# Local attention: the inverse roots on ScalarE and GpSimd without powers, and half of the probabilities' division on GpSimd

## What is computed

```
qkv = shift_token(x) @ wqkv
q, k, v = split(qkv, 3)                      # 8 heads of 64
q = q / clip(norm(q), 1e-12) * q_scale
k = k / clip(norm(k), 1e-12) * k_scale
q, k = rotary_xpos(q, k)                     # q * cos * s + rotate_half(q) * sin * s, k with 1 / s
sim = (q * 8) @ k.T  for windows of 64 queries, 128 keys (the window and the one before)
attn = softmax(where(mask, -max, sim))
x = x + (attn @ v) @ wo
```

## Time and profile before

| | us |
|---|---|
| median of 3 runs (790.19 to 793.98) | 792.9 |
| the profiled execution | 794.17 |
| its span, first to last instruction | 792.4 |
| mean granted TensorE clock, share of full speed | 0.938 |

### The profile page before, as it was taken

One profiled execution on the slowest core, in us unless ns is written; L12 is line 12 of the kernel. 1 busy time (PEld: TensorE's weight loads), 2 busy tenths in 40 slices (PEclk: granted clock), 3 DMA queues, 4 the chain that ended last, 5 costly groups with the idle time before them and its releaser, 6 DMA issues. The chain is left out here.

```text
span 792.4 us, 15860 instructions
## 1 busy us (share of the span) xinstructions
PE 630.7 (80%) x5506; PEld 438.3 (55%) x5539; DVE 569.8 (72%) x1440; ACT 489.6 (62%) x1423; POOL 391.0 (49%) x436
## 2 busy tenths in 40 slices
PE   1747778778999986986899998699699999997242
PEld 0425555345666664553567666555477777776112
DVE  2454666878999974645999998555577777777396
ACT  1524666576889973324989998432577777774243
POOL 6626665798999941109999997010101111111202
PEclk9887999999999999998999999999999999998665
DMA  6700000001001001011001101000000000000001
GB/s 201 163 1 1 1 1 1 8 21 22 22 22 34 22 22 58 1 27 24 22 21 28 23 22 25 11 1 1 1 1 2 1 1 3 1 2 1 1 0 53
DMA packets 20218, 17.26 MB, mean 22 GB/s; under 512 B 7234, under 2 KB 15884, under 8 KB 20044
## 3 DMA queue, kind: packets, MB, share of 16 engines
q1 hardware_dynamic: 20140, 16.26, 8.3%
HBM read 8.91 MB, written 1.05 MB: 13 GB/s over the span
## 5 line engine op out<-in xcount | busy, mean ns | idle before, releaser
L1131 ACT ACTIVATE pc<-PS,nb,rsq 128x128 f32<-128x128 f32 x256 | 114.1, 464 | 2.7 <-DVE nb L1469 2.1
L761 PE MATMUL PS<-wqkv,hB 128*128 128x512 f32 x192 | 104.9, 631 | 8.0 <-DVE rsin L1455 4.8
L1189 ACT ACTIVATE pc<-PS,nb 128x256 f32<-128x256 f32 x128 | 59.0, 473 | 45.0 <-DVE nb L1619 45.0
L450 POOL TENSOR_TENSOR rsk<-btmp,neghalf 128x8 f32<-128x8 f32 x32 | 60.5, 1890 | 5.9 <-POOL btmp L445 5.9
L769 PEld LDWEIGHTS PS<-ident,rot 128*128 128x128 f32 x256 | 31.6, 143 | 53.1 <-issue 33.7
L1619 DVE TENSOR_REDUCE nb<-PS 128x2 f32<-128x512 f32 x64 | 40.8, 680 | 25.0 <-PE PS L943 25.0
L450 POOL TENSOR_TENSOR rsq<-btmp,neghalf 128x8 f32<-128x8 f32 x32 | 53.1, 1661 | 6.2 <-POOL btmp L445 6.2
L1478 DVE TENSOR_TENSOR pc<-pc,rden 128x512 f32<-128x512 f32 x64 | 53.8, 841 | 2.2
L555 POOL TENSOR_TENSOR rot<-rot,rsin 128x512 f32<-128x512 f32 x32 | 40.6, 1270 | 27.1 <-DVE rsin L1455 27.1
L1131 ACT ACTIVATION_READ_ACCUMULATOR pc<-PS,nb,rsq 128x1 f32 x256 | 53.8, 210 | 0.0
L769 PE MATMUL PS<-ident,rot 128*128 128x128 f32 x256 | 39.7, 279 | 16.7 <-POOL rot L561 16.2
(11 more groups left out here) (226 smaller groups left out, 1717.8 us busy)
## 6 DMA issues: line engine op xcount, KB each, us to landing
V<-V SPq DMA_DIRECT2D x48, 128.0 KB, 2.2
wqkv<-in_L_ffn_wqkv SPq DMA_DIRECT2D x2, 768.0 KB, 5.0
out<-x SPq DMA_DIRECT2D x4, 256.0 KB, 2.3
x<-in_x SPq DMA_DIRECT2D x1, 768.0 KB, 5.4
ctxT<-in_ctxT SPq DMA_DIRECT2D x1, 768.0 KB, 7.3
w<-in_L_ffn_w SPq DMA_DIRECT2D x2, 341.0 KB
ctxs<-in_ctx SPq DMA_DIRECT2D x1, 576.0 KB, 6.5
gel<-in_bands SPq DMA_DIRECT2D x1, 512.0 KB, 7.1
```

Source lines behind the costliest of these rows:

```text
L450: return tt(dst, tmp, neghalf[:, 0, 0:tmp.shape[1]], ALU.pow)
L761: i = mm(ps, hB[:, b % 2, j * P:(j + 1) * P], wqkv[:, w * INNER:(w + 1) * INNER], start=True, stop=True)
L1131: i = af(pc[:, g % 2, par, c * P:(c + 1) * P], c_bank(g, par)[:, c * P:(c + 1) * P], ACT.Exp, bias=nb[:, g % 2, at], scale=rsq[:, g % 8, 2 ...
L1189: i = af(pc[:, u % 2, par, n * S:(n + 1) * S], c_bank(u, par)[:, n * S:(n + 1) * S], ACT.Exp, bias=nb[:, u % 2, par * 2 + n:par * 2 + n + ...
```

## The change

It does five things, all in local attention. (1) The clip of the sums of squares is done for q and k at once (128x16), and ahead of both rotary sums; GpSimd waits for both sums of squares there. (2) ScalarE takes logarithm and exponential, exp(-0.5 ln s), in place of the power (`b_roots`), and GpSimd refines the result by one Newton step of four small operations, then makes the k product. (3) The division of the odd bank's probabilities moves from VectorE to GpSimd (`b_normalise`), behind `b_turned` in each step; VectorE keeps the reciprocal. (4) The order of pieces and of VectorE's and ScalarE's jobs in a step is changed: k, t, q ahead of the scores, kT, v, W, qT behind, the even bank ahead of the odd one, sums of squares ahead of the rotary products. (5) ScalarE loads one table set with logarithm and exponential at its start and at the start of layer 1.

```diff
-B_MID = ["t", "k", "kT"]
-B_END = ["v", "qT", "q", "W"]
+B_MID = ["k", "t", "q"]
+B_END = ["kT", "v", "W", "qT"]
 @@ GpSimd
             def b_turned(g):
-                _, k, turn = b_piece("k", g)
-                pool.wait_ge(bank_free[k], 2 * turn + 2)
-                r = rot[:, g % 2 * 2, :]
-                tt(r, r, rsin[:, 0, :], ALU.add).then_inc(sem("B_ksum"), 1)
                 pool.wait_ge(sem("B_kss"), g + 1)
-                rsqrt(rsk[:], ss[:, g % 2, 0, :], btmp[:, 0, :], 1e-24, ALU.max, "B_ktmp", g + 1).then_inc(sem("B_krs"), 1)
+                pool.wait_ge(sem("B_qss"), g + 1)
+                sg, r = ss[:, g % 2], rsqk[:, g % 8]
+                ts(sg, sg, 1e-24, None, ALU.max).then_inc(sem("B_clip"), 1)
+                for name in ("k", "q"):
+                    _, k, turn = b_piece(name, g)
+                    pool.wait_ge(bank_free[k], 2 * turn + 2)
+                    m = rot[:, g % 2 * 2 + int(name == "q"), :]
+                    tt(m, m, rsin[:, int(name == "q"), :], ALU.add).then_inc(sem("B_ksum" if name == "k" else "B_q"), 1)
+
+                pool.wait_ge(sem("B_root"), 2 * g + 2)
+                tt(root[:, 0], r, r, ALU.mult).then_inc(sem("B_newton"), 1)
+                pool.wait_ge(sem("B_newton"), 4 * g + 1)
+                tt(root[:, 1], root[:, 0], sg, ALU.mult).then_inc(sem("B_newton"), 1)
+                pool.wait_ge(sem("B_newton"), 4 * g + 2)
+                ts(root[:, 0], root[:, 1], -0.5, 1.5, ALU.mult, ALU.add).then_inc(sem("B_newton"), 1)
+                pool.wait_ge(sem("B_newton"), 4 * g + 3)
+                tt(r, r, root[:, 0], ALU.mult).then_inc(sem("B_newton"), 1)
+                pool.wait_ge(sem("B_newton"), 4 * g + 4)
                 pool.wait_ge(sem("B_ksum"), g + 1)
...
+                r3 = rot[:, g % 2 * 2, :].rearrange("p (h d) -> p h d", h=H)
+                tt(r3, r3, rsqk[:, g % 8, 0, :].unsqueeze(2).broadcast_to([P, H, DH]), ALU.mult).then_inc(sem("B_k"), 1)
+
+            def b_normalise(g):
+
+                pool.wait_ge(b_rden[1], g + 1)
+                e = pc[:, g % 2, 1, :].rearrange("p (n k) -> p n k", n=4)
+                tt(e, e, rden[:, g % 2, 4:8].unsqueeze(2).broadcast_to([P, 4, P]), ALU.mult).then_inc(p_full[1], 1)
+
+            def b_step(layer, step):
+
+                if 0 <= step + B_AHEAD["k"] < T:
+                    b_turned(layer * T + step + B_AHEAD["k"])
+                if 0 <= step + 1 < T:
+                    b_normalise(layer * T + step + 1)
 @@ ScalarE
+            nc.scalar.preload_act_table_set("natural_log_exp_and_others")
             act.wait_ge(sem("ld_A"), A_LOADS * 16)
...
+            def b_roots(g):
+
+                r = rsqk[:, g % 8]
+                act.wait_ge(sem("B_clip"), g + 1)
+                af(r, ss[:, g % 2], ACT.Ln).then_inc(sem("B_root"), 1)
+                act.wait_ge(sem("B_root"), 2 * g + 1)
+                af(r, r, ACT.Exp, scale=-0.5).then_inc(sem("B_root"), 1)
 @@ ScalarE, b_step
-                if ahead:
-                    b_exps(g + 1, 1)
                 if 0 <= step < T:
                     for par in range(2):
                         b_copy(g, par)
-                pieces("k", "t")
+                pieces("k")
                 if ahead:
                     b_exps(g + 1, 0)
-                pieces("kT", "v", "qT", "q")
+                pieces("q", "t")
+                if ahead:
+                    b_exps(g + 1, 1)
+                pieces("kT")
+                if 0 <= step + B_AHEAD["q"] < T:
+                    b_roots(g + B_AHEAD["q"])
+                pieces("v", "qT")
 
             for layer in range(DEPTH):
                 if layer:
+                    nc.scalar.preload_act_table_set("natural_log_exp_and_others")
 @@ VectorE: in b_turned the sum of squares (red, L1458) moves ahead of the two products
 @@ VectorE, b_scale
-                nc.vector.reciprocal(rden[:, g % 2, at], den[:, g % 2, at]).then_inc(sem("B_rden"), 1)
-                dve.wait_ge(sem("B_rden"), g * 2 + 2 - par)
+                nc.vector.reciprocal(rden[:, g % 2, at], den[:, g % 2, at]).then_inc(b_rden[par], 1)
+                if par:
+                    return
+                dve.wait_ge(b_rden[0], g + 1)
 @@ VectorE, b_step
+                if 0 <= step + B_AHEAD["k"] < T:
+                    b_turned(0, g + B_AHEAD["k"])
+                if 0 <= step + 1 < T:
+                    b_scale(g + 1, 0)
+                if 0 <= step + B_AHEAD["q"] < T:
+                    b_turned(1, g + B_AHEAD["q"])
                 if 0 <= step + 1 < T:
                     b_scale(g + 1, 1)
-                if 0 <= step + B_AHEAD["k"] < T:
-                    b_turned(0, g + B_AHEAD["k"])
                 if 0 <= step + 2 < T:
-                    b_max(g + 2, 1)
-                if 0 <= step + 1 < T:
-                    b_scale(g + 1, 0)
-                if 0 <= step + 2 < T:
-                    b_max(g + 2, 0)
+                    for par in range(2):
+                        b_max(g + 2, par)
                 if 0 <= step < T:
                     b_outputs(g)
-                if 0 <= step + B_AHEAD["q"] < T:
-                    b_turned(1, g + B_AHEAD["q"])
```

More of the change, by code:

```diff
@@ L226, in program @@
         rs = sb("rs", [P, 4])
-        rsq = sb("rsq", [P, 8, H])
-        rsk = sb("rsk", [P, H])
+        rsqk = sb("rsqk", [P, 8, 2, H])
+        root = sb("root", [P, 2, 2, H])
         av = sb("av", [P, 3, 10 * D])
@@ L294, in program @@
         bank_full, bank_free = ([sem("bank_%s%d" % (name, k)) for k in range(3)] for name in ("full", "free"))
+        b_rden = [sem("B_rden%d" % par) for par in range(2)]
         b_v2 = [sem("B_v2_%d" % k) for k in range(4)]
@@ L550, in b_turned @@
             def b_turned(g):
-                _, k, turn = b_piece("k", g)
-                pool.wait_ge(bank_free[k], 2 * turn + 2)
-                r = rot[:, g % 2 * 2, :]
-                tt(r, r, rsin[:, 0, :], ALU.add).then_inc(sem("B_ksum"), 1)
                 pool.wait_ge(sem("B_kss"), g + 1)
-                rsqrt(rsk[:], ss[:, g % 2, 0, :], btmp[:, 0, :], 1e-24, ALU.max, "B_ktmp", g + 1).then_inc(sem("B_krs"), 1)
-                pool.wait_ge(sem("B_ksum"), g + 1)
-                pool.wait_ge(sem("B_krs"), g + 1)
@@ L574, in _ @@
                         a_step(u)
-                        if 0 <= u - A_UNITS + B_AHEAD["k"] < T:
-                            b_turned(u - A_UNITS + B_AHEAD["k"])
-                else:
-                    for t in range(T):
-                        b_turned(layer * T + t)
+                        b_step(0, u - A_UNITS)
+                else:
+                    for step in B_STEPS:
+                        b_step(layer, step)
                 def f_copy(g):
@@ L1131, in b_exps @@
                     i = af(pc[:, g % 2, par, c * P:(c + 1) * P], c_bank(g, par)[:, c * P:(c + 1) * P], ACT.Exp,
-                           bias=nb[:, g % 2, at], scale=rsq[:, g % 8, 2 * c + par:2 * c + par + 1], accum_out=den[:, g % 2, at])
+                           bias=nb[:, g % 2, at], scale=rsqk[:, g % 8, 1, 2 * c + par:2 * c + par + 1], accum_out=den[:, g % 2, at])
                 i.then_inc(e_full[par], 1)
@@ L1450, in b_turned @@
                 dve.wait_ge(sem("B_%ssq" % name), g + 1)
+                red(ss[:, g % 2, which, :], sq[:, which, :].rearrange("p (h d) -> p h d", h=H), AXX, ALU.add) \
+                    .then_inc(sem("B_%sss" % name), 1)
                 tt(rot[:, g % 2 * 2 + which, :].rearrange("p (h d) -> p h d", h=H), ps.rearrange("p (h d) -> p h d", h=H),
@@ L1457, in b_turned @@
                    ALU.mult).then_inc(bank_free[k], 2)
-                red(ss[:, g % 2, which, :], sq[:, which, :].rearrange("p (h d) -> p h d", h=H), AXX, ALU.add) \
-                    .then_inc(sem("B_%sss" % name), 1)
             def b_max(g, par):
@@ L1466, in b_max @@
                     .then_inc(sem("B_mx"), 1)
-                dve.wait_ge(sem("B_mx"), g * 2 + 2 - par)
-                dve.wait_ge(sem("B_qrs"), g + 1)
-                tt(nb[:, g % 2, at], mx[:, g % 2, at], rsq[:, g % 8, par::2], ALU.mult).then_inc(nb_full[par], 1)
+                dve.wait_ge(sem("B_mx"), g * 2 + par + 1)
+                dve.wait_ge(sem("B_newton"), 4 * g + 4)
+                tt(nb[:, g % 2, at], mx[:, g % 2, at], rsqk[:, g % 8, 1, par::2], ALU.mult).then_inc(nb_full[par], 1)
             def b_scale(g, par):
```

## The result

The changed kernel takes 879.7 us (median of 4, 877.05 to 882.04) against 792.9 us before: ratio 1.107, 95% interval 1.102 to 1.111. It is slower by 87 us; the forecast was 875, inside 848 to 900. The profiled execution took 878.1 us, its span is 876.3 against 792.4.

What follows compares the result with a forecast made beforehand. GpSimd was taken to set the rate, 8.45 us a tile. With steps of 12.4 us, layer 1 +44.7, layer 0 +38.1, edges +1.2 and table -1.3 gave +82.7 us on the 792.9 us median: 875 us, range 848 to 900.

Steps and rivals of the forecast that it cites:

- The ring: In full local-attention steps, the odd turn waits for GpSimd's division, queued behind its wait for tile g+4: 11.9 us a step.
- The clock: TensorE's idle gap in each ring step makes some matmuls run slow: +0.5 us a step, bounds 0 and 1.3.
- rival (b): TensorE's clock stays slow through all of the ring: 24x0.8 us more, 895 us; chance 0.08.
- The shared port: VectorE with two SBUF inputs and a reading GpSimd exclude each other; VectorE's products nb wait, but the sum is unchanged.
- The edges: Filling and draining of both local layers: 2x(1.1-0.5) = +1.2 us, with the early table load -1.3 us.
- draining: Last three steps of each local layer, without b_turned: 6.2 us each, 18.6 against 19.1 us, so -0.5.
- overlap of layer 0 with the first attention, 0 with +-5: Where layer 0 overlaps the first attention, steps take about 10 us either way: no change, within 5 us.
- the prediction's 10, 19 and 5 us: Upward uncertainties used for the range: Newton's operation times 10 us, the slow clock +19, layer 0's overlap +-5.
- (a): The ring without a slow clock: 24 steps of 11.9 us, 863 us; chance 0.77 together with the forecast.
- (c): Every logarithm and exponential on ScalarE loads its table: 48 us longer, 923 us; chance 0.03.
- (d): The ring has misread slack, 3.5 of 6.3 us hidden; ScalarE's 8.2 us then bounds a step: 774 us; chance 0.05.
- (e): Half of the slack in the ring is hidden: a period of 10.5 us, 830 us; chance 0.07.

## Why the prediction was right, and where it wasn't

**The ring** (its main step) was right in kind and in size. Forecast 11.9 us without the clock, measured 11.57; clip at 5.60, measured 5.63. The differences are in the Newton step, 1.19 for 1.35, since an operation takes 0.22 for 0.24 and the gap ahead of the product is 0.08 for 0.15, in the clip, 0.20 for 0.26, and in the handover from GpSimd to TensorE, 0.05 (473.51 - 472.42 - 1.04) for the 0.15 that the earlier trace rows gave. TensorE is idle for 2.8 us ahead of a turn, a little under the 3 us that the prediction named as a sign.

**The clock** was right in kind: 0.41 us a step on average for a forecast of 0.5, and the repeated transposes show that the idle gap causes it. It also settles rival (b): the clock isn't slow throughout.

**The shared port** is off the ring, as forecast. In the step shown above, VectorE's product nb that starts at 469.48, inside GpSimd's sums of 467.77 to 470.27, takes 0.81 us; the next one, outside them, takes 0.16. None of the ring's waits names it. The port comes onto the path, as far as I found, only in the run with q's sum of squares last and the division on VectorE, where that division holds up the clip.

**Sizes that were off.** With a step of 12.4 for a measured 12.0 the two layers were put 10 us too high. The edges were put 11 us too low: 5.4 in the start, 1.8 in the filling of layer 1, 3.7 in the draining. The term that failed is "overlap of layer 0 with the first attention, 0 with +-5". The trace of the changed kernel shows what it left out (timeline of all engines):

```profile
139.58 0.21 ACT L1148 ACTIVATE rsqk<-ss 128x16 f32<-128x16 f32 x1 [1.54 <-POOL ss L556]
...
142.01 1.09 PE L732 MATMUL PS<-pT,av 128*64 128x128 f32 x16 [2.71 <-ACT pT L1095]
...
147.98 1.92 PE L778 MATMUL PS<-wqkv,hB 128*128 128x512 f32 x2
```

ScalarE waits for the clip, the first attention's copies come late, TensorE idles for 2.7 us, and two of the next projections then run at the lower clock (2.07 and 1.92 us, the latter as in the earlier trace rows). The turn after comes 16.2 us later (136.79 to 152.99), 10.8 before. Every profiled kernel with the roots on ScalarE has 16 us or more there; the kernel before with the early table alone has 10.8. From the turn at 129.40 to tile 0's odd turn it is 9.8 us more than before; the start had gained 4.6 us, some by the table and the rest by a clock that fell elsewhere in this one execution. So the edges' 11 us too little and the layers' 10 us too much cancelled, and the closeness of 875 to 880 is partly luck: the ring itself accounts for 72.8 us of the 83.9. The upper end of the range isn't the sum of its parts either: 875 and the prediction's 10, 19 and 5 us make 909, not 900.

**Draining** was put at 18.6 and took 19.7 and 21.2. The last two steps are 6.3 and 6.2 us, as forecast, but the first of the three takes 7.2 and 8.7.

**The rivals.** (a) and the forecast were the case. (c), the table not kept, is ruled out: beside the start one load stands ahead of each layer or stage that changes the set, none between logarithm and exponential, which follow each other in 0.26 us. (d) and (e), slack in the ring, did not occur; but (d)'s price was too good for the kernel that it describes: once the ring is cut, the step is 8.54, not 8.2, and the best time is 787, not 774.

## What to carry to other kernels

When a job moves to another in-order engine, write down what stands ahead of it in that engine's queue, and follow each of these waits back: if one leads to the job's own consumer one step earlier, the step can't be shorter than the way round, however idle the engines are. The cure is to split the moved work so that the short thing somebody waits for goes first, and to give the buffers inside the loop a second copy: here the same instructions gave 880, 822, 810 and, with one more buffer, 787 us. And before taking work off one of several engines that are nearly full, look at what stands next to it: some 2.4 us less on GpSimd went with 0.04 us less in a full step.

## What the runs showed of the hardware

- GpSimd does an elementwise operation on 128x16 in 0.20 to 0.24 us, a power on 128x8 in 1.66: the price is the power, not the instruction.
- Idling ahead of a turn lowers TensorE's clock for matmuls that are on the path. With gaps of 2.8 us the middle of layer 1 had 0.93 and some steps took 12 to 12.9 us, with 1.6 us (450 to 530 us of the run without Newton) or 1.1 us 1.00 and equal steps. Work of no use in the gap (16 transposes a step) brought every full step of the ring to 11.57 us.
- A small GpSimd operation can be held up by a VectorE operation that began just before it: the clip took 0.75 us behind a division that had started 0.05 us earlier, and 0.24 us when it started first. The division took 0.69 us both times.
- ScalarE's logarithm and exponential on 128x16 take 0.22 us each, and exponentials under the joint table set cost the same as under the other, 462 ns for 464.
